# Scores of the second layer from fp16 halves of q and k, and the block of v ahead of the output block

## The chip, the cores and the metric

The kernel runs on one core of a Trainium2 chip. The engines that matter are TensorE (PE in the profile, PEld for its weight loads), VectorE (DVE), ScalarE (ACT), GpSimd (POOL) and SyncE (SP), whose queue issues every DMA. Each engine takes its own instructions strictly in the order in which they were written down and waits on semaphores for the others. The metric is the device time of one execution in microseconds (us); lower is better.

## The reference

128 graphs of 128 nodes with 512 features pass through two layers. Layer 0 is a graph layer with eight heads, which the change doesn't touch. Layer 1, which it does, is masked attention with four heads of 64 columns:

```python
h = jnp.maximum(_layernorm(x, axis=-1), 0.0)
q = split_heads(h @ Wq); k = split_heads(h @ Wk); v = split_heads(h @ Wv)
sim = jnp.einsum('bhid,bhjd->bhij', q, k) * scale
sim = jnp.where(adjacency_mask[:, None, :, :], sim, neg)
attn = jax.nn.softmax(sim, axis=-1)
out = jnp.einsum('bhij,bhjd->bhid', attn, v)
x = x + (out @ Wo + bo)
```

## The kernel before

`layer0` runs first and leaves its result in DRAM (`x_scratch`); `layer1` follows. In the profile its tiles carry the prefix `l_`.

A product of two float32 matrices is made from fp16 halves: each operand is scaled by a power of two and stored as a high half and the rest as a low half, and `split_products` adds high by high, high by low and low by high. The scores of layer 1 were the exception: `qk_copy` evicted q and k as float32 (`q_sb`, `k_sb`, scaled back by `unscale`), and `scores` (L1419) multiplied them as float32, four matmuls a graph, each for one head in half of the array's rows.

`layer1` goes over the graphs in one software-pipelined loop, written out by hand in each engine's own order. One step n handles several graphs at once:

- PE: `project_qk(n+4)`, 12 matmuls of 512 columns into `ps_pj[0]`, in turn a pair of heads of q or of k for a group of four graphs; `project_out(n-4)`, 6 matmuls of 512 columns; `scores(n+1)`; `project_v(n+4)`, 12 of 256 columns; `weigh_values(n-2)`, 12 small ones (L1432).
- ACT: `qk_copy(n+4)` (L1216 or L1218), `relu(n+10)` (L1204), `h_high(n+10)` (L1209), `exps(n+1)` (four exponentials with their sums, L1230), `v_high(n+4)` (L1224), `aT_high(n-2)` (L1242), `p_high(n+1)` (L1237).
- DVE: `add_residual(n-4)` (L1330), `row_max(n+1)` (four masked reductions in L121), `stats(n+15)` (L85, L87), `normalise(n+1)` (a reciprocal, L1311, and the product with it, L1313), `v_low(n+4)` (L1300), `aT_low(n-2)` (L1323), `p_low(n+1)` (L1318).
- POOL: `h_low(n+9)` (L1166), `add_bias(n-3)` (L1173), and in one step of four each `factors` (seventeen small operations, L102 to L105 with L74 to L80 between) and `convert_mask` (L1159).
- SP: `transpose_h(n+9)` (L1108), `transpose_p(n)` (L1115), the load of x for graph n+17 (L1098), in one step of four a load of masks (L1140), and `store(n-5)` (L1102). In steps with n%4 = 3 the transpose of p goes ahead of that of h.

`add_residual(n)` writes `o_sb[:, n % 2]` and so waits until the store of graph n-2 has landed. `ps_pj[0]`, `ps_pj[1]`, `ps_s`, `ps_av` and `ps_o` have one buffer each. The next block of q or k waits until the one before has left `ps_pj[0]`.

Of the kernel before, what the change touches and what calls it, by code (L numbers as in the profile page):

```python
# [26 lines left out]
HB = 4  # L27
# [89 lines left out]
def mask_scores(nc, dve, s_ready, n, masked, scores, mask, negmax):  # L117

    dve.wait_ge(s_ready, n)
    for i in range(HB):  # L120
        last = nc.vector.tensor_tensor_reduce(masked[:, i], scores[:, i // 2, (i % 2) * P:(i % 2 + 1) * P], mask, -1.0,  # L121
                                              FLOAT_MAX, ALU.add, ALU.min, negmax[:, i:i + 1])
    return last
# [44 lines left out]
def layer0(nc, next_layer, next_weights, x, adj, map_w, map_wT, map_b, q_wT, q_b, k_wT, k_b, gmap_w, gmap_b, gcn_WT, x1):  # L168

    with ExitStack() as ctx:  # L170
# [449 lines left out]
        def _(dve):  # L620
# [387 lines left out]
def layer1(nc, prepared, x1, adj, bo, out):  # L1008


    with ExitStack() as ctx:
# [6 lines left out]
        def sem(name):  # L1018
# [12 lines left out]
        q_sb = sb("q_sb", [P, 2, PAIRS1, QUAD * P])  # L1031
        k_sb = sb("k_sb", [P, 2, PAIRS1, QUAD * P])
# [15 lines left out]
        nprobs = sb("nprobs", [P, HB, P])  # L1048
# [24 lines left out]
        relu_done, hhi_done, q_done, k_done, vhi_done, exp_done, phi_done, ahi_done = act_sems = [  # L1073
            sem(n) for n in ("relu_done", "hhi_done", "q_done", "k_done", "vhi_done", "exp_done", "phi_done", "ahi_done")]
        hlo_done, vlo_done, negmax_done, rec_done, np_done, plo_done, alo_done, out_done = dve_sems = [
            sem(n) for n in ("hlo_done", "vlo_done", "negmax_done", "rec_done", "np_done", "plo_done", "alo_done", "out_done")]
        mask_ready, res_ready = pool_sems = [sem("mask_ready"), sem("res_ready")]
# [71 lines left out]
        def _(pool):  # L1149
# [25 lines left out]
            factors(QUAD)  # L1175
            convert_mask(0)
# [19 lines left out]
        def _(act):  # L1196
# [14 lines left out]
            def qk_copy(i):  # L1211

                g, c = divmod(i, QUAD)
                act.wait_ge(qk_ready, count(i + 1))
                if c % 2 == 0:
                    nc.scalar.activation(q_sb[:, g % 2, c // 2], ps_pj[0][:], ACT.Copy, scale=unscale["q"]).then_inc(q_done, 1)  # L1216
                else:
                    nc.scalar.activation(k_sb[:, g % 2, c // 2], ps_pj[0][:], ACT.Copy, scale=unscale["k"]).then_inc(k_done, 1)  # L1218
# [15 lines left out]
            def p_high(n):  # L1234
                act.wait_ge(np_done, count(n + 1))
                act.wait_ge(pT_loaded[n % 2], 16 * (n // 2))
                nc.scalar.activation(p16[:, n % 2, 0], nprobs[:], ACT.Copy, scale=F16_SCALE).then_inc(phi_done, 1)  # L1237
# [15 lines left out]
            act.wait_ge(scale_chain, SCALE_STEPS * len("qkvo") + 2)  # L1253
            for c in range(QUAD):
                qk_copy(c)
                v_high(c)
                relu(QUAD + c)
                h_high(QUAD + c)
# [6 lines left out]
            for n in range(B):  # L1265
                if n + QUAD < B:
                    qk_copy(n + QUAD)
# [5 lines left out]
                if n + QUAD < B:  # L1273
                    v_high(n + QUAD)
# [8 lines left out]
        def _(dve):  # L1283
# [12 lines left out]

            def v_low(i):
# [4 lines left out]
            def row_max(n):  # L1302
                if n % QUAD == 0:
# [3 lines left out]
                            negmax[:, n % 2]).then_inc(negmax_done, 1)  # L1307
# [8 lines left out]
            def p_low(n):  # L1316
                dve.wait_ge(phi_done, count(n + 1))
                nc.vector.scalar_tensor_tensor(p16[:, n % 2, 1], nprobs[:], F16_SCALE, p16[:, n % 2, 0], ALU.mult,  # L1318
                                               ALU.subtract).then_inc(plo_done, 1)
# [24 lines left out]
            nc.vector.tensor_tensor(unscale["o"], unscale["o"], unscale["v"], ALU.mult).then_inc(scale_chain, 1)  # L1344
            for n, k in enumerate("qkvo"):
# [3 lines left out]
            dve.wait_ge(scale_chain, SCALE_STEPS * len("qkvo") + 2)  # L1349
            for i in range(QUAD, 2 * QUAD):  # L1350
                stats(i)
            for j in range(QUAD):
                v_low(j)
# [3 lines left out]
            p_low(0)  # L1357
# [25 lines left out]
        def _(pe):  # L1383
# [3 lines left out]
            def project_qk(i):  # L1387
# [4 lines left out]

                if c % 2 == 0:
                    pe.wait_ge(k_done, count(2 * g + c // 2))
                else:
                    pe.wait_ge(q_done, count(2 * g + c // 2 + 1))
# [12 lines left out]
            def scores(n):  # L1409
                g, j = divmod(n, QUAD)  # L1410
                cols = slice(j * P, (j + 1) * P)
                if j == 0:
                    pe.wait_ge(q_done, count(2 * g + 2))
                    pe.wait_ge(k_done, count(2 * g + 2))
# [42 lines left out]
            for n in range(B):  # L1457
                if n + QUAD < B:
                    project_qk(n + QUAD)
                if n >= 4:  # L1460
# [3 lines left out]
                if n + QUAD < B:  # L1464
                    project_v(n + QUAD)
# [52 lines left out]
```

## Time and profile before

| | us |
|---|---|
| time, median of 3 runs | 2706.66 (2703.7 to 2708.87) |
| the profiled execution, its own time | 2705.26 |
| its span | 2703.5 |
| PE busy in the span | 2603.0 (96%) |
| DVE busy | 1982.0 (73%) |
| ACT busy | 1752.0 (65%) |
| POOL busy | 1404.3 (52%) |

The span is the time between the first and the last instruction that the profiler saw. A busy PE is not one at its peak. The mean over the span mixes both layers; layer 1 begins at about 1814 us and its steady part fills the stretch from about 1885 to 2665 us.

### The profile page before, as it was taken

To read this page: it belongs to the slowest core of one execution; us is meant where nothing else is said; L and a number is where in the kernel's file an instruction comes from. 1 tells how busy PE (TensorE), PEld (TensorE's weight loads), DVE (VectorE), ACT (ScalarE), POOL (GpSimd) and SP (SyncE) were. 2 spreads that over 40 slices of the span, in tenths; PEclk is the share of its full clock that TensorE was granted. 3 is DMA by queue.
4 is the path that set the end of the run, shared out by engine and by line. 5 is a ranking of instruction groups with operands and counts; after the bars stand their busy time and mean duration, and the time that the engine had idled before them with its cause. 6 is when DMAs were issued, how large, how long until landed. Compare 5 with 4: busy or idle time off the path is not lost. (4 is left out here: it accounts for less than half of the span.)

```text
span 2703.5 us, 62497 instructions
## 1 busy us (share of the span) xinstructions
PE 2603.0 (96%) x20886; PEld 1401.6 (52%) x20886; DVE 1982.0 (73%) x6359; ACT 1752.0 (65%) x5020; POOL 1404.3 (52%) x2798
## 2 busy tenths in 40 slices
PE   6999999999999999999999999947999999999998
PEld 3455555555555555555555555534555555555554
DVE  5487777777777877777777778755777777777765
ACT  3466666666666666666666666645777777777774
POOL 4255555455545555555555455514655556565552
PEclk8999999999999999999999999968999999999998
DMA  4257666766766676667666766575777778777763
GB/s 139 60 129 151 146 132 142 152 134 134 144 148 136 132 150 149 128 132 157 141 134 140 154 129 130 120 175 113 158 165 159 172 164 167 164 159 171 159 144 90
DMA packets 944336, 385.33 MB, mean 143 GB/s; under 512 B 857488, under 2 KB 859024, under 8 KB 944016
## 3 DMA queue, kind: packets, MB, share of 16 engines
q1 hardware_dynamic: 944016, 381.34, 66.2%
q8 instruction: 167, 2.74, 0.4%
q14 instruction: 153, 1.25, 0.1%
HBM read 112.76 MB, written 67.11 MB: 67 GB/s over the span
## 5 line engine op out<-in xcount | busy, mean ns | idle before, releaser
L534 ACT ACTIVATE probs<-probs,negmax 128x128 f32<-128x128 f32 x1024 | 398.2, 390 | 468.3 <-DVE negmax L121 468.3
L445 POOL TENSOR_TENSOR o_sb<-o_sb,xres 128x512 f32<-128x512 f32 x128 | 162.7, 1271 | 503.6 <-DVE o_sb L694 498.3
L163 PE MATMUL ps_pj<-wm_hi,hT 128*128 128x512 f16 x1024 | 325.1, 379 | 4.1 <-DVE m_sb L637 4.1
L163 PE MATMUL ps_pj<-wv_hi,hT 128*128 128x512 f16 x1024 | 326.4, 380 | 0.0
L163 PE MATMUL ps_pj<-hT,wk_hi 128*128 128x512 f16 x1024 | 305.8, 380 | 0.0
L163 PE MATMUL ps_pj<-hT,wq_hi 128*128 128x512 f16 x1024 | 305.3, 380 | 0.0
L1230 ACT ACTIVATE l_probs<-l_probs,l_negmax 128x128 f32<-128x128 f32 x512 | 199.1, 390 | 152.9 <-DVE l_negmax L121 152.9
L1166 POOL TENSOR_TENSOR l_h<-l_h 128x512 f16<-128x512 f32 x124 | 143.5, 1158 | 269.4 <-ACT l_h L1209 157.8
L121 DVE CUSTOM_DVE_ANT_0 probs<-ps_sc,mask 128x128 f32<-128x128 f32 x1024 | 235.4, 284 | 53.2 <-PE ps_sc L899 52.5
L676 DVE SCALAR_TENSOR_TENSOR c<-cprobs,c 128x512 f16<-128x512 f32 x256 | 182.9, 714 | 80.9 <-ACT c L541 80.8
L541 ACT ACTIVATE c<-cprobs 128x512 f16<-128x512 f32 x256 | 160.3, 626 | 118.4 <-DVE cprobs L670 114.7
L1173 POOL TENSOR_TENSOR l_xres<-room,l_bo_rows 128x512 f32<-128x512 f32 x124 | 169.2, 1364 | 63.4 <-DVE l_o_sb L1330 63.2
L670 DVE SCALAR_TENSOR_TENSOR cprobs<-ps_sc,bound,probs 128x512 f32<-128x512 f32 x256 | 189.1, 739 | 16.4 <-ACT probs L534 13.1
L632 DVE TENSOR_TENSOR h<-h 128x512 f16<-128x512 f32 x128 | 109.0, 851 | 122.2 <-ACT h L500 122.1
L892 PEld LDWEIGHTS ps_sc<-room 64*128 64x128 f32 x2048 | 135.9, 188 | 116.0 <-issue 115.8
L892 PE MATMUL ps_sc<-room 64*128 64x128 f32 x2048 | 185.2, 300 | 9.7 <-DVE cprobs L670 9.2
L163 PE MATMUL ps_pj<-hT,wq_lo 128*128 128x512 f16 x512 | 194.3, 379 | 0.0
L163 PE MATMUL ps_pj<-hT,wk_lo 128*128 128x512 f16 x512 | 194.0, 379 | 0.0
L163 PE MATMUL ps_pj<-wv_lo,hT 128*128 128x512 f16 x512 | 194.0, 379 | 0.0
L163 PE MATMUL ps_pj<-wm_lo,hT 128*128 128x512 f16 x512 | 194.0, 379 | 0.0
L163 PE MATMUL l_ps_pj<-l_wv_hi,l_hT 128*128 128x256 f16 x1024 | 190.5, 274 | 2.6 <-DVE l_v_lo L1300 2.5
L534 ACT ACTIVATION_READ_ACCUMULATOR probs<-probs,negmax 128x1 f32 x1024 | 191.0, 186 | 0.0
(197 smaller groups left out, 6675.8 us busy)
## 6 DMA issues: line engine op xcount, KB each, us to landing
xg<-in_x SPq DMA_DIRECT2D x128, 256.0 KB, 3.3
xres<-in_x SPq DMA_DIRECT2D x128, 256.0 KB, 3.0
x_scratch<-o_sb SPq DMA_DIRECT2D x128, 256.0 KB, 2.4
out<-l_o_sb SPq DMA_DIRECT2D x128, 256.0 KB, 3.3
room<-x_scratch SPq DMA_DIRECT2D x124, 256.0 KB, 3.1
cpT<-c SPq DMA_TRANSPOSE x256, 3.2
mask_u<-in_adj SPq DMA_DIRECT2D x32, 64.0 KB, 2.4
hT<-h SPq DMA_TRANSPOSE x128, 3.3
```

Of the source, the lines that this page charges most:

```text
L121: last = nc.vector.tensor_tensor_reduce(masked[:, i], scores[:, i // 2, (i % 2) * P:(i % 2 + 1) * P], mask, -1.0, FLOAT_MAX, ALU.add, ALU. ...
L163: last = pe.matmul(out, a(kt), b(kt), start=(n == 0), stop=(n == 3 * kts - 1))
L445: nc.gpsimd.tensor_tensor(o_sb[:, j % 2], o_sb[:, j % 2], xres[:, j % 2], ALU.add).then_inc(res_done, 1)
L534: last = nc.scalar.activation(probs[:, i], probs[:, i], ACT.Exp, bias=negmax[:, u % 2, i:i + 1], scale=-1.0, accum_out=zsum[:, u % 4, hh:h ...
L541: nc.scalar.activation(c16[:, n % 2, 0], cprobs[:], ACT.Copy, scale=F16_SCALE).then_inc(cph_done, 1)
L632: nc.vector.tensor_tensor(h16[:, j % 2, D:], h32[:, j % 2], h16[:, j % 2, 0:D], ALU.subtract).then_inc(hlo_done, 1)
L670: nc.vector.scalar_tensor_tensor(cprobs[:].rearrange("p (b h) n -> p b (h n)", b=2), ps_c[n % 2], bound[:, t % 2, j:j + 1], probs[:].rearr ...
L676: nc.vector.scalar_tensor_tensor(c16[:, n % 2, 1], cprobs[:], F16_SCALE, c16[:, n % 2, 0], ALU.mult, ALU.subtract).then_inc(cpl_done, 1)
L892: nc.tensor.matmul(ps_s[n % 2][:, b, pl * P:(pl + 1) * P], q_sb[rows, t % 2, pr, cols], k_sb[rows, t % 2, pr, cols], start=True, stop=True)
L1166: nc.gpsimd.tensor_tensor(h16[:, i % 2, D:], h32[:, i % 2], h16[:, i % 2, 0:D], ALU.subtract).then_inc(hlo_done, 1)
L1173: nc.gpsimd.tensor_tensor(xres[:, i % 2], row(i), bo_rows[:], ALU.add).then_inc(res_ready, 1)
L1230: last = nc.scalar.activation(probs[:, hh], probs[:, hh], ACT.Exp, bias=negmax[:, n % 2, hh:hh + 1], scale=-1.0, accum_out=zsum[:, n % 2, ...
```

## The change

Scores are made from fp16 halves. `qk_high` (ACT) writes the high half of a block of q or k as it stands in PSUM, `qk_low` (DVE) the rest, and `scores` issues twelve fp16 matmuls for the four float32 ones. The scale moves into `mask_scores`, where `score_scale` takes the place of -1.0, and into the mask, which now holds 0 or the scaled constant `excluded`. The next block on PE waits for `qk_low` (`qklo_done`) and no more for the copy.

`project_v`, `v_high` and `v_low` move: on PE ahead of `project_out`, on ACT ahead of `relu`, on DVE ahead of `add_residual`, right behind `qk_low`. `p_low` moves from DVE to POOL, behind `add_bias`. `normalise` gets one small operation more (it scales the sums before the reciprocal), `nprobs` a second buffer.

```diff
-                nc.gpsimd.tensor_scalar(mask[:, t % 2], mask_u8[:, t % 2], -NEG1, NEG1, ALU.mult, ALU.add).then_inc(mask_ready, 1)
+                nc.gpsimd.tensor_scalar(mask[:, t % 2], mask_u8[:, t % 2], -1.0, excluded[:, 0:1], ALU.add, ALU.mult).then_inc(mask_ready, 1)
@@ POOL
+            def p_low(n):
+                pool.wait_ge(phi_done, count(n + 1))
+                nc.gpsimd.tensor_tensor(p16[:, n % 2, 1], nprobs[:, n % 2], p16[:, n % 2, 0], ALU.subtract).then_inc(plo_done, 1)
...
                 if n >= 3:
                     add_bias(n - 3)
+                p_low(n)
                 if n % QUAD == 1 and n + 11 < B:
                     factors(n + 11)
@@ ACT
+                nc.scalar.copy(qk_hi["qk"[c % 2]][:, g % 2, c // 2], ps_pj[0][:]).then_inc(qkhi_done, 1)
...
             for n in range(B):
                 if n + QUAD < B:
-                    qk_copy(n + QUAD)
+                    qk_high(n + QUAD)
+                    v_high(n + QUAD)
                 if n + 10 < B:
                     relu(n + 10)
                     h_high(n + 10)
                 if n + 1 < B:
                     exps(n + 1)
-                if n + QUAD < B:
-                    v_high(n + QUAD)
@@ DVE
+            def qk_low(i):
+                g, c = divmod(i, QUAD)
+                kind = "qk"[c % 2]
+                dve.wait_ge(qkhi_done, count(i + 1))
+                nc.vector.tensor_tensor(qk_lo[kind][:, g % 2, c // 2], ps_pj[0][:], qk_hi[kind][:, g % 2, c // 2],
+                                        ALU.subtract).then_inc(qklo_done, 1)
...
             def normalise(n):
                 dve.wait_ge(exp_done, count(n + 1))
-                nc.vector.reciprocal(rec[:], zsum[:, n % 2]).then_inc(rec_done, 1)
-                dve.wait_ge(rec_done, count(n + 1))
-                nc.vector.tensor_tensor(nprobs[:], probs[:], rec[:].unsqueeze(2).to_broadcast([P, HB, P]),
+                dve.wait_ge(plo_done, count(n - 1))
+                nc.vector.tensor_scalar(rec[:], zsum[:, n % 2], 1.0 / F16_SCALE, None, ALU.mult).then_inc(rec_done, 1)
+                dve.wait_ge(rec_done, count(2 * n + 1))
+                nc.vector.reciprocal(rec[:], rec[:]).then_inc(rec_done, 1)
+                dve.wait_ge(rec_done, count(2 * n + 2))
+                nc.vector.tensor_tensor(nprobs[:, n % 2], probs[:], rec[:].unsqueeze(2).to_broadcast([P, HB, P]),
                                         ALU.mult).then_inc(np_done, 1)
...
             for n in range(B):
+                if n + QUAD < B:
+                    qk_low(n + QUAD)
+                    v_low(n + QUAD)
                 if n >= 4:
                     add_residual(n - 4)
...
                 if n + 1 < B:
                     normalise(n + 1)
-                if n + QUAD < B:
-                    v_low(n + QUAD)
                 if n >= 2:
                     aT_low(n - 2)
-                if n + 1 < B:
-                    p_low(n + 1)
@@ PE
-                if c % 2 == 0:
-                    pe.wait_ge(k_done, count(2 * g + c // 2))
-                else:
-                    pe.wait_ge(q_done, count(2 * g + c // 2 + 1))
+                pe.wait_ge(qklo_done, count(i))
...
                 for pr in range(PAIRS1):
-                    for b in range(2):
-                        rows = slice(DH * b, DH * b + DH)
-                        mm = nc.tensor.matmul(ps_s[:, b, pr * P:(pr + 1) * P], q_sb[rows, g % 2, pr, cols], k_sb[rows, g % 2, pr, cols],
-                                              start=True, stop=True)
+                    for i, (q_part, k_part) in enumerate(((qk_hi, qk_hi), (qk_hi, qk_lo), (qk_lo, qk_hi))):
+                        for b in range(2):
+                            rows = slice(DH * b, DH * b + DH)
+                            mm = nc.tensor.matmul(ps_s[:, b, pr * P:(pr + 1) * P], q_part["q"][rows, g % 2, pr, cols],
+                                                  k_part["k"][rows, g % 2, pr, cols], start=(i == 0), stop=(i == 2))
...
             for n in range(B):
                 if n + QUAD < B:
                     project_qk(n + QUAD)
+                if n + QUAD < B:
+                    project_v(n + QUAD)
                 if n >= 4:
                     project_out(n - 4)
                 if n + 1 < B:
                     scores(n + 1)
-                if n + QUAD < B:
-                    project_v(n + QUAD)
```

The set-up of layer 1 gains three small DVE operations for `score_scale` and `excluded`, for which POOL waits ahead of its first mask.

## Rows read from the trace of the kernel before

The numbers of graphs and steps follow from the code; the stretch is steady, and its steps repeat.

**Rows 1.** Windows: stretch, its length; busy PE, PEld, DVE, ACT, POOL; clock, DMA share, GB/s.

```profile
...
1850.00:1880.00 30.00, 20.82 (x125) 10.78 (x122) 16.41 (x60) 18.95 (x55) 16.45 (x42) 0.83 0.63 126
2300.00:2400.00 100.00, 100.00 (x782) 56.80 (x782) 72.92 (x248) 72.02 (x212) 59.08 (x103) 1.00 0.78 164
```

**Rows 2.** Chain that ended last, 2300 to 2330: start us, us, what.

```profile
...
2299.98 0.65 PE l_ps_s L1419 x8
2300.62 1.42 PE l_ps_pj L163 x12
2302.04 0.46 PE l_ps_av L1432 x12
2302.50 2.70 PE l_ps_pj L163 x12
2305.19 1.29 PE l_ps_o L163 x6
2306.49 0.65 PE l_ps_s L1419 x8
```

**Rows 3.** Timeline of DVE: start us, us, instruction, [idle before <-releaser].

```profile
...
2308.16 0.75 DVE L1330 SCALAR_TENSOR_TENSOR l_o_sb<-l_ps_o,l_w_st,l_xres 128x512 f32<-128x512 f32 x1 [2.41 <-DMA out<-l_o_sb]
2308.83 0.28 DVE L121 CUSTOM_DVE_ANT_0 l_probs<-l_ps_s,l_mask 128x128 f32<-128x128 f32 x1
...
2311.46 0.18 DVE L1311 RECIPROCAL l_rec<-l_zsum 128x4 f32<-128x4 f32 x1 [0.89 <-ACT l_probs L1230]
2311.68 0.69 DVE L1313 TENSOR_TENSOR l_nprobs<-l_probs,l_rec 128x512 f32<-128x512 f32 x1
2312.28 0.42 DVE L1300 TENSOR_TENSOR l_v_lo<-l_ps_pj,l_v_hi 128x256 f16<-128x256 f32 x1
2312.62 0.42 DVE L1323 SCALAR_TENSOR_TENSOR l_aT_lo<-l_ps_av,l_aT_hi 128x256 f16<-128x256 f32 x1
2313.06 0.69 DVE L1318 SCALAR_TENSOR_TENSOR l_p<-l_nprobs,l_p 128x512 f16<-128x512 f32 x1
2313.67 0.75 DVE L1330 SCALAR_TENSOR_TENSOR l_o_sb<-l_ps_o,l_w_st,l_xres 128x512 f32<-128x512 f32 x1
...
2317.19 1.06 DVE L1313 TENSOR_TENSOR l_nprobs<-l_probs,l_rec 128x512 f32<-128x512 f32 x1
```

**Rows 4.** Timeline of ACT, same stretch.

```profile
...
2309.78 0.40 ACT L1230 ACTIVATE l_probs<-l_probs,l_negmax 128x128 f32<-128x128 f32 x1 [2.51 <-DVE l_negmax L121]
...
2311.34 0.35 ACT L1224 CAST l_v_hi<-l_ps_pj 128x256 f16<-128x256 f32 x1
...
2312.40 0.63 ACT L1237 ACTIVATE l_p<-l_nprobs 128x512 f16<-128x512 f32 x1 [0.44 <-DVE l_nprobs L1313]
2312.94 0.67 ACT L1218 ACTIVATE l_k_sb<-l_ps_pj,l_w_st 128x512 f32<-128x512 f32 x1
2313.51 0.80 ACT L1204 ACTIVATE l_h<-room,ln_st 128x512 f32<-128x512 f32 x1
```

**Rows 5.** Waits of DVE, 2100 to 2500: total us, times, longest.

```profile
...
DVE l_o_sb L1330 <- DMA out<-l_o_sb: 38.2, 23, 3.1
```

**Rows 6.** Timeline of POOL, same stretch as 3.

```profile
...
2310.65 0.20 POOL L102 TENSOR_TENSOR ln_st<-ln_st,l_consts 128x4 f32<-128x4 f32 x1 [0.33 <-DVE ln_st L87]
...
2316.54 1.16 POOL L1166 TENSOR_TENSOR l_h<-l_h 128x512 f16<-128x512 f32 x1 [0.18 <-POOLq L108]
2317.66 1.72 POOL L1173 TENSOR_TENSOR l_xres<-room,l_bo_rows 128x512 f32<-128x512 f32 x1
...
2322.04 1.27 POOL L1173 TENSOR_TENSOR l_xres<-room,l_bo_rows 128x512 f32<-128x512 f32 x1
```

**Rows 7.** Timeline of the DMA queue on SP.

```profile
...
2304.71 0.42 SPq L1102 DMA_DIRECT2D out<-l_o_sb  x1
...
2313.78 1.23 SPq L1115 DMA_TRANSPOSE l_pT<-l_p  x1
...
2315.69 0.42 SPq L1102 DMA_DIRECT2D out<-l_o_sb  x1
```

More of the change, by code:

```diff
@@ L114, in slot, with mask_scores @@
     return 2 * (hh % 2) + hh // 2
-def mask_scores(nc, dve, s_ready, n, masked, scores, mask, negmax):
+def mask_scores(nc, dve, s_ready, n, masked, scores, mask, negmax, scale):
     dve.wait_ge(s_ready, n)
     for i in range(HB):
-        last = nc.vector.tensor_tensor_reduce(masked[:, i], scores[:, i // 2, (i % 2) * P:(i % 2 + 1) * P], mask, -1.0,
+        last = nc.vector.tensor_tensor_reduce(masked[:, i], scores[:, i // 2, (i % 2) * P:(i % 2 + 1) * P], mask, scale,
                                               FLOAT_MAX, ALU.add, ALU.min, negmax[:, i:i + 1])
@@ L1030, in layer1 @@
         bo_rows = sb("bo_rows", [P, D])
-        q_sb = sb("q_sb", [P, 2, PAIRS1, QUAD * P])
-        k_sb = sb("k_sb", [P, 2, PAIRS1, QUAD * P])
+        qk_hi = {k: sb(f"{k}_hi", [P, 2, PAIRS1, QUAD * P], F16) for k in "qk"}
+        qk_lo = {k: sb(f"{k}_lo", [P, 2, PAIRS1, QUAD * P], F16) for k in "qk"}
+        score_scale = sb("score_scale", [P, 1])
+        excluded = sb("excluded", [P, 1])
         v_hi = sb("v_hi", [P, 2, QUAD, INNER], F16)
@@ L1047, in layer1 @@
         probs = sb("probs", [P, HB, P])
-        nprobs = sb("nprobs", [P, HB, P])
+        nprobs = sb("nprobs", [P, 2, HB, P])
         p16 = sb("p16", [P, 2, 2, HB, P], F16)
@@ L1072, in layer1 @@
             sem(n) for n in ("qk_ready", "vp_ready", "s_ready", "av_ready", "o_ready")]
[L1073 to L1077, printed above, removed]
+        relu_done, hhi_done, qkhi_done, vhi_done, exp_done, phi_done, ahi_done = act_sems = [
+            sem(n) for n in ("relu_done", "hhi_done", "qkhi_done", "vhi_done", "exp_done", "phi_done", "ahi_done")]
+        hlo_done, qklo_done, vlo_done, negmax_done, rec_done, np_done, alo_done, out_done = dve_sems = [
+            sem(n) for n in ("hlo_done", "qklo_done", "vlo_done", "negmax_done", "rec_done", "np_done", "alo_done", "out_done")]
+        mask_ready, res_ready, plo_done = pool_sems = [sem("mask_ready"), sem("res_ready"), sem("plo_done")]
+        SCALE_OPS = SCALE_STEPS * len("qkvo") + 5
         adjt = adj.rearrange("(g j) p d -> g p j d", j=QUAD)
@@ L1209, in h_high, with qk_high @@
                 nc.scalar.copy(h16[:, i % 2, 0:D], h32[:, i % 2]).then_inc(hhi_done, 1)
-            def qk_copy(i):
+            def qk_high(i):
                 g, c = divmod(i, QUAD)
                 act.wait_ge(qk_ready, count(i + 1))
-                if c % 2 == 0:
-                    nc.scalar.activation(q_sb[:, g % 2, c // 2], ps_pj[0][:], ACT.Copy, scale=unscale["q"]).then_inc(q_done, 1)
-                else:
-                    nc.scalar.activation(k_sb[:, g % 2, c // 2], ps_pj[0][:], ACT.Copy, scale=unscale["k"]).then_inc(k_done, 1)
+                nc.scalar.copy(qk_hi["qk"[c % 2]][:, g % 2, c // 2], ps_pj[0][:]).then_inc(qkhi_done, 1)
             def v_high(i):
@@ L1236, in p_high @@
                 act.wait_ge(pT_loaded[n % 2], 16 * (n // 2))
-                nc.scalar.activation(p16[:, n % 2, 0], nprobs[:], ACT.Copy, scale=F16_SCALE).then_inc(phi_done, 1)
+                nc.scalar.activation(p16[:, n % 2, 0], nprobs[:, n % 2], ACT.Copy).then_inc(phi_done, 1)
             def aT_high(n):
@@ L1252, in _ @@
                 nc.scalar.activation(w_hi[k][:], raw[k], ACT.Copy, scale=w_st[:, n, 2:3]).then_inc(prep_hi, 1)
-            act.wait_ge(scale_chain, SCALE_STEPS * len("qkvo") + 2)
             for c in range(QUAD):
-                qk_copy(c)
+                qk_high(c)
                 v_high(c)
@@ L1306, in row_max @@
                 mask_scores(nc, dve, s_ready, count(n + 1), probs, ps_s, mask[:, n // QUAD % 2, n % QUAD],
-                            negmax[:, n % 2]).then_inc(negmax_done, 1)
+                            negmax[:, n % 2], score_scale[:, 0:1]).then_inc(negmax_done, 1)
             def normalise(n):
                 dve.wait_ge(exp_done, count(n + 1))
-                nc.vector.reciprocal(rec[:], zsum[:, n % 2]).then_inc(rec_done, 1)
-                dve.wait_ge(rec_done, count(n + 1))
-                nc.vector.tensor_tensor(nprobs[:], probs[:], rec[:].unsqueeze(2).to_broadcast([P, HB, P]),
+                dve.wait_ge(plo_done, count(n - 1))
[4 more added lines that the diff above has]
+                nc.vector.tensor_tensor(nprobs[:, n % 2], probs[:], rec[:].unsqueeze(2).to_broadcast([P, HB, P]),
                                         ALU.mult).then_inc(np_done, 1)
[L1316 to L1319, printed above, removed]
             def aT_low(n):
@@ L1352, in _ @@
             for j in range(QUAD):
+                qk_low(j)
                 v_low(j)
@@ L1356, in _ @@
             normalise(0)
-            p_low(0)
             for i in range(3 * QUAD, 15):
```

14 lines of the change are left out of this document (8 added, 6 removed).

## The prediction

> **What bounds the kernel now.** I read the windows first, for the stage that the change touches. In a steady stretch of layer 1 PE is busy all the time at the full granted clock, the other engines between 59 and 73% [rows 1]. The chain that ended last then stays on PE for whole steps: scores 0.65, the block of v 1.42, the weighing of values 0.46, the block of q or k 2.70, the output block 1.29. From scores to scores it is 2306.49 - 2299.98 = 6.51 us [rows 2]. PE is the bound there, and only there can the reader believe that cheaper matmuls pay.
>
> A bound by one busy engine hides loops in which several engines wait for each other in turn. So I looked next at DVE and ACT, in their timelines, for the shortest step that they can make. From the `add_residual` at 2308.16, which a store had held up, to the next at 2313.67 DVE needed 5.51 us and waited only for ACT's exponentials [rows 3]. That is a loop: add_residual, row_max, exps, normalise, p_high, p_low, add_residual. It lies 1.00 us under PE's step, and that slack is what swallows the waits for stores, 38.2 us in some 61 steps [rows 5]. Whether the change keeps this slack is the question.
>
> **PE's step after it.** Four float32 matmuls of scores, 0.65 us, become twelve fp16 ones of 128 columns. The nearest row from below is the weighing of values, also twelve of 128 columns in halves of the array: 0.46. From above, without any overlap of the halves: the output block's 6 x 512 columns in 1.29 us make 0.054 us for 128 columns, and twelve of them 0.65, as now [rows 2]. I take 0.46, since it is the same number and size of instructions. The order on PE changes no sum, except that the pause of about 0.1 us around the change to half-array matmuls may go. So PE's own step becomes 6.2 to 6.5 us; I take 6.3. Alone this would give (6.51 - 6.3) x 120 = 25 us. 120 is the number of steps with a block of q or k, 124, less some four of the ramp.
>
> **The loop through ACT and DVE after it.** In the new order ACT runs p_high(n), then qk_high(n+4); DVE's first work of the step is qk_low(n+4), which waits for it, and v_low, add_residual and row_max(n+1) are queued behind it. So the eviction of q and k and its low half come into the loop, and so does v_low, which before was done behind normalise while ACT made p_high. Only p_low leaves it. Start to start, from [rows 3, 4]:
>
> - p_high to qk_high: 0.54 (2312.40 to 2312.94).
> - qk_high to qk_low: 0.70. The eviction takes 0.67, and p_high's end to the start of p_low was 0.03.
> - qk_low to v_low: 0.67. The trace has no such operation. From below 0.61, a subtraction or product of 512 columns in SBUF (nprobs at 2311.68 to v_lo at 2312.28); from above 0.67, one of 512 columns out of PSUM (o_sb at 2308.16 to 2308.83). It reads PSUM, so 0.67.
> - v_low to add_residual: 0.34 (2312.28 to 2312.62). v_high is long done: it starts 0.57 after qk_high and takes 0.35, so it ends 0.92 after it, and v_low starts 1.37 after it.
> - add_residual to row_max: 0.67.
> - row_max to exps: 0.95 (2308.83 to 2309.78).
> - exps to DVE's first operation of normalise: 1.68 (2309.78 to 2311.46).
> - The added small operation and its wait: 0.22, as the reciprocal beside it (2311.46 to 2311.68); a second 0.22 for the reciprocal.
> - nprobs to p_high: 0.72 (2311.68 to 2312.40).
>
> The sum is 0.54 + 0.70 + 0.67 + 0.34 + 0.67 + 0.95 + 1.68 + 0.22 + 0.22 + 0.72 = 6.71 us. It is over PE's 6.3 and over the 6.51 of today, so the loop is the new bound and PE idles some 0.4 us a step. What stats, aT_low, relu and h_high cost stays hidden: stats behind the exponentials, aT_low behind p_high and qk_high, relu and h_high behind qk_low to row_max. The bounds of the loop are 6.60 (0.61 for qk_low, and 0.05 less for a plain copy, as p_high's 0.63 against 0.67) and 6.75.
>
> **What p_low on POOL does.** POOL was busy 59.08 in 100 us [rows 1], 3.85 a step; 1.16 more, the time of h_low, makes 5.0, so it doesn't become the bound. But one step in four it is late. Take a step n with n%4 = 1 and count from the start of p_high(n). p_low(n) runs from 0.66 to 1.82. The factors take 2316.54 - 2310.65 = 5.89 up to the next h_low [rows 6], so h_low starts at 7.76, add_bias at 8.88, p_low(n+1) at 10.18, and it ends at 11.34, where it was due at 6.71 + 1.82 = 8.53. On SP the transpose of p, the load and then the store are queued behind it; from the start of such a transpose to that of the store it is 2315.69 - 2313.78 = 1.91, and a store lands 2308.16 - 2304.71 = 3.45 after its start, which is when the waiting add_residual began [rows 3, 7]. So the store of graph n-4 has landed at 11.37 + 1.91 + 3.45 = 16.7. add_residual(n-2), which needs its buffer, is due two loops later at 2 x 6.71 + 0.54 + 0.70 + 0.67 + 0.34 = 15.7. A stall of 1.0 us in four steps, 0.25 a step, now with no slack to swallow it. In step n+2 the transpose of h goes behind that of p: p_low(n+2) ends at 16.0, two transposes of some 1.5 and a load of 0.6 bring the store to 19.6, landed at 23.1, and it is needed at 3 x 6.71 + 1.0 + 2.25 = 23.4. So there is no second stall, by 0.3 us. The moved block of v helps here: the transpose of h waited for it at times, and it now comes early. Bounds: 0 if stores land 1 us sooner, and 0.5 a step if a second step stalls too.
>
> **POOL beside DVE.** nprobs took 1.06 us in place of 0.69 while POOL's h_low and add_bias ran [rows 3, 6]. Late POOL work will meet one nprobs in four; 0.1 to 0.4 us each, so 0.05 a step. p_low itself meets qk_low and add_residual.
> The Trainium skill (SBUF — State Buffer, "Who interferes with whom") says that a DVE instruction with two SBUF inputs and a GpSimd instruction that reads SBUF take one read interface in turns, the second blocked until the first ends. By that rule nprobs would wait out up to 0.8 us of an h_low once in four steps, 0.2 a step in place of 0.05, and the time would be 18 us more, 2787. The row shows less, 0.37 in one nprobs.
>
> **The sum.** 6.71 + 0.25 + 0.05 = 7.01 us a step, 0.50 more than 6.51, x 120 = 60 us. Ramp and tail: PE waits for qk_low in the first group (about 0.2 x 3), the first p_low on POOL is 0.5 longer; the last steps lose v_low and p_low from their loop. Together +2, an estimate. The profiled execution's 2705.3 becomes 2767; the median is 1.4 above that execution, so 2769 us.
>
> **Rivals.**
> - The loop alone: no stall by stores, because they land sooner or POOL's lateness shrinks in the longer step. 6.60 to 6.75, x 120 and +2: 2720 to 2738 us. For it: the DMA share of 0.78 would fall, and the stall hangs on 1 us. Chance 0.23.
> - More stalls: the second store too, or nprobs blocked for a whole POOL operation, 7.2 to 7.4 a step: 2791 to 2815. PE's clock is part of this case: in the ramp, where PE waited, the granted clock was 0.83 [rows 1], and a stall of 1 us atop the 0.4 of idle could bring it down. Against: PE has slack then. Chance 0.15.
> - Faster. The loop does not bind, and PE's shorter step shows: 6.2 to 6.3, so 25 to 37 us less, 2670 to 2682. It decides at a loop under 6.5; that needs the qk part (0.54 + 0.70 + 0.67) to be dearer on paper than on the chip by 0.2 or more, if p_high and qk_high overlap further, say. Against it: each link is a start-to-start time out of the trace and each engine keeps its order. Chance 0.07.
> - No change: the loop comes out at 6.5 by small errors of both signs. 0.05.
> - The fp16 scores could also gain nothing (0.65). With the loop as bound this moves nothing.
>
> **How the numbers follow.** The forecast, loop with one stall, has 0.50: 2750 to 2790. I take 0.2% (5.4 us) as what can be told from no change. Slower: 0.50 + 0.23 + 0.15 = 0.88; same 0.05; faster 0.07. The range leaves out the faster and equal cases and the top of the third: 2720 to 2800.
>
> **What would show it.** In the changed profile PE is below 95% busy in steady windows and waits ahead of the q and k blocks for `qk_low`. DVE's steps without a stall are 6.7 us from add_residual to add_residual, with the waits for qk_high and for the exponentials in each. Behind each group of factors p_low on POOL comes late, and two steps on add_residual waits about 1 us for the DMA. Scores take 0.46. Steps of 6.2 to 6.3 with PE at 100% would prove the loop wrong; steps of 6.7 without the DMA wait would prove the stall wrong; qk_low much above 0.75 us would push the time over the range.

## The result

The changed kernel took 2781.44 us (2777.6 to 2789.28, six runs) against 2707.45 (2703.7 to 2709.93, six runs): a ratio of 1.0279, 95% interval 1.0267 to 1.0291. It is slower by 74 us, where 62 had been forecast (2769, range 2720 to 2800).

The windows of the changed kernel come first (stretch and length; busy PE, PEld, DVE, ACT, POOL; granted clock, DMA share, GB/s):

```profile
...
1850.00:1880.00 30.00, 20.89 (x150) 11.12 (x149) 15.76 (x55) 17.18 (x46) 14.81 (x39) 0.89 0.59 127
2300.00:2400.00 100.00, 90.18 (x770) 51.03 (x770) 73.43 (x248) 65.42 (x200) 67.55 (x115) 1.00 0.73 150
```

PE, which was busy without a pause [rows 1], is now busy for 90 of 100 us. No other engine is full. The time went into waits between engines. How long a step is now, read from `add_residual` to `add_residual` in DVE's timeline over 108 steps, from the first of these rows to the second:

```profile
...
1952.83 0.75 DVE L1339 SCALAR_TENSOR_TENSOR l_o_sb<-l_ps_o,l_w_st,l_xres 128x512 f32<-128x512 f32 x1
```

```profile
...
2723.91 0.74 DVE L1339 SCALAR_TENSOR_TENSOR l_o_sb<-l_ps_o,l_w_st,l_xres 128x512 f32<-128x512 f32 x1
```

(2723.91 - 1952.83) / 108 = 7.14 us. The same measure on the kernel before gives (2645.71 - 1941.87) / 108 = 6.52. The difference over 120 steps is 75 us; the two spans differ by 77.9. So the loss lies in the steady steps, and only 3 us elsewhere.

PE's own step did get shorter, as its timeline shows in a stretch in which PE was catching up after a wait and had none of its own (rows left out between are of the same blocks):

```profile
...
2299.89 0.60 PE L163 MATMUL l_ps_pj<-l_hT,l_wk_hi 128*128 128x512 f16 x2
...
2303.80 0.38 PE L163 MATMUL l_ps_o<-l_wo_hi,l_aT_hi 128*128 128x512 f16 x1
...
2305.19 0.23 PE L1427 MATMUL l_ps_s<-l_k_hi,l_q_hi 64*128 64x128 f16 x2
...
2305.63 0.30 PE L1440 MATMUL l_ps_av<-l_pT,l_v_hi 128*64 128x128 f16 x4
...
2306.09 0.61 PE L163 MATMUL l_ps_pj<-l_hT,l_wq_hi 128*128 128x512 f16 x2
```

From one block of k to the next block of q it is 2306.09 - 2299.89 = 6.20 us, and the twelve fp16 score matmuls hold PE for 2305.63 - 2305.19 = 0.44, where the float32 ones held it for 0.65 [rows 2]. That explains 0.21 of the 0.31 by which 6.20 is shorter than 6.51. The other 0.10 comes with the order of the blocks: e5 below has the new order with float32 scores and a median of 6.40 from block to block of q and k, e9 to e11 have fp16 scores with other orders and 6.30. What holds the step is on DVE and ACT. First DVE in a plain step:

```profile
...
2305.87 0.74 DVE L1339 SCALAR_TENSOR_TENSOR l_o_sb<-l_ps_o,l_w_st,l_xres 128x512 f32<-128x512 f32 x1
2306.53 0.34 DVE L121 CUSTOM_DVE_ANT_0 l_probs<-l_ps_s,l_mask,l_score_scale 128x128 f32<-128x128 f32 x1
...
2309.40 0.17 DVE L1323 TENSOR_SCALAR l_rec<-l_zsum 128x4 f32<-128x4 f32 x1 [0.89 <-ACT l_probs L1236]
2309.61 0.18 DVE L1325 RECIPROCAL l_rec<-l_rec 128x4 f32<-128x4 f32 x1
2309.82 0.69 DVE L1327 TENSOR_TENSOR l_nprobs<-l_probs,l_rec 128x512 f32<-128x512 f32 x1
2310.43 0.42 DVE L1332 SCALAR_TENSOR_TENSOR l_aT_lo<-l_ps_av,l_aT_hi 128x256 f16<-128x256 f32 x1
2311.68 0.69 DVE L1305 TENSOR_TENSOR l_q_lo<-l_ps_pj,l_q_hi 128x512 f16<-128x512 f32 x1 [0.84 <-ACT l_q_hi L1224]
2312.29 0.41 DVE L1311 TENSOR_TENSOR l_v_lo<-l_ps_pj,l_v_hi 128x256 f16<-128x256 f32 x1
2312.62 0.74 DVE L1339 SCALAR_TENSOR_TENSOR l_o_sb<-l_ps_o,l_w_st,l_xres 128x512 f32<-128x512 f32 x1
```

and ACT in the same step:

```profile
...
2307.72 0.40 ACT L1236 ACTIVATE l_probs<-l_probs,l_negmax 128x128 f32<-128x128 f32 x1 [1.19 <-DVE l_negmax L121]
...
2310.55 0.63 ACT L1243 ACTIVATE l_p<-l_nprobs 128x512 f16<-128x512 f32 x1 [0.91 <-DVE l_nprobs L1327]
2311.08 0.57 ACT L1224 CAST l_q_hi<-l_ps_pj 128x512 f16<-128x512 f32 x1
2311.55 0.38 ACT L1230 CAST l_v_hi<-l_ps_pj 128x256 f16<-128x256 f32 x1
```

From 2305.87 to 2312.62 it is 6.75 us. Going through the links in the order of the prediction: p_high to qk_high 0.53, to qk_low 0.60, to v_low 0.61, to add_residual 0.33, to row_max 0.66 (2305.87 to 2306.53), row_max to exps 1.19, exps to the small operation 1.68, then 0.21, 0.21 and 0.73. The sum is 6.75. DVE waits only for ACT in it (0.89 and 0.84) and ACT only for DVE (1.19 and 0.91), so there is no slack left in the loop.

The four steps of a group are not alike. In means over 27 groups they last 6.77, 6.76, 7.67 and 7.36 us; before it was 5.66, 6.39, 6.30 and 7.71, in which the shorter steps made up for the long one while PE went on without a pause. The third step is long by one instruction, in 23 of the 27 groups `nprobs`, in three the small operation ahead of it; the last group, shown further down, has neither. DVE:

```profile
...
2316.62 1.53 DVE L1327 TENSOR_TENSOR l_nprobs<-l_probs,l_rec 128x512 f32<-128x512 f32 x1
...
2320.26 0.74 DVE L1339 SCALAR_TENSOR_TENSOR l_o_sb<-l_ps_o,l_w_st,l_xres 128x512 f32<-128x512 f32 x1
```

nprobs takes 1.53 us in place of 0.69. POOL at that time:

```profile
...
2311.03 1.16 POOL L1169 TENSOR_TENSOR l_h<-l_h 128x512 f16<-128x512 f32 x1 [0.18 <-POOLq L108]
2312.15 1.29 POOL L1180 TENSOR_TENSOR l_xres<-room,l_bo_rows 128x512 f32<-128x512 f32 x1
2313.40 1.16 POOL L1174 TENSOR_TENSOR l_p<-l_nprobs,l_p 128x512 f16<-128x512 f32 x1
2314.54 0.69 POOL L1162 TENSOR_SCALAR l_mask<-l_mask_u,l_excluded 128x512 bf16<-128x512 uint8 x1
2315.20 1.16 POOL L1169 TENSOR_TENSOR l_h<-l_h 128x512 f16<-128x512 f32 x1
2316.31 1.29 POOL L1180 TENSOR_TENSOR l_xres<-room,l_bo_rows 128x512 f32<-128x512 f32 x1
```

The factors ended at 2311, and six operations follow without a gap, the last an `add_bias` from 2316.31 to 2317.60. nprobs started at 2316.62 and ended at 2318.15, 0.55 after POOL was done. As it takes 0.69 otherwise, it had done at most 0.14 of its work before. In means over the 27 third steps nprobs is 0.71 longer and the small operation 0.17, together 0.88 of the 0.91 by which that step exceeds a plain one.

The fourth step is long, 7.3 us or more, in 16 of 27 groups. The waits from 2100 to 2500 us (56 steps, 14 groups; total us, times, longest) name the place:

```profile
...
PE l_ps_s L1427 <- DVE l_k_lo L1305: 32.6, 14, 2.7
...
DVE l_o_sb L1339 <- DMA out<-l_o_sb: 3.5, 5, 1.1
DVE l_o_sb L1339 <- PE l_ps_o L163: 2.8, 6, 0.5
```

PE waits 2.3 us a group ahead of the scores of a new group, because these need the last low half of k, made in the same step. What follows, on PE (idle time ahead in brackets):

```profile
...
2461.82 0.23 PE L1427 MATMUL l_ps_s<-l_k_hi,l_q_hi 64*128 64x128 f16 x2 [2.27 <-DVE l_k_lo L1305]
...
2462.25 0.30 PE L1440 MATMUL l_ps_av<-l_pT,l_v_hi 128*64 128x128 f16 x4
...
2462.71 0.67 PE L163 MATMUL l_ps_pj<-l_hT,l_wq_hi 128*128 128x512 f16 x2
...
2463.60 1.06 PE L163 MATMUL l_ps_pj<-l_hT,l_wq_hi 128*128 128x512 f16 x2
...
2466.16 0.79 PE L163 MATMUL l_ps_pj<-l_hT,l_wq_hi 128*128 128x512 f16 x2
```

and in a window of 2 us of it (PEclk, the granted clock, is the first figure behind the busy times):

```profile
...
2464.00:2466.00 2.00, 2.00 (x6) 0.76 (x5) 1.01 (x5) 1.78 (x9) 1.16 (x1) 0.50 1.16 39
```

Two matmuls of the block of q take 1.06 us, where they took 0.60 above, at a granted clock of 0.50, the lower of PE's two levels (1.2 in place of 2.4 GHz), behind a wait of 2.27 us. (The DMA share, the next figure, reads above 1 in so short a window; nothing here rests on it.) Its eviction is not late yet, but the block of v and the output block behind it are, and `add_residual` pays:

```profile
...
2462.01 0.74 DVE L1339 SCALAR_TENSOR_TENSOR l_o_sb<-l_ps_o,l_w_st,l_xres 128x512 f32<-128x512 f32 x1
...
2469.81 0.75 DVE L1339 SCALAR_TENSOR_TENSOR l_o_sb<-l_ps_o,l_w_st,l_xres 128x512 f32<-128x512 f32 x1 [0.47 <-PE l_ps_o L163]
```

2469.81 - 2462.01 = 7.80 us. This does not happen in every group. PE waits 2.25 us or more in 26 of 27, but only in 11 of them did the granted clock fall, between 0.3 us ahead of the wait's end and 1.4 us behind it. Behind a wait of 2.27 us that ended at 2089.36 it stayed at 1.00, and that fourth step took 6.75. In nine of the eleven `add_residual` waited for the output block, and those steps last 7.68 in the mean. In seven other groups it waited for a store, and they last 7.86. The remaining eleven last 6.75 to 6.96. So the 0.60 by which the mean fourth step exceeds a plain one is made in about equal parts by PE's late blocks behind the wait and by stores.

The last of the 27 groups is a group without POOL's factors, since none are left to make. DVE, and PE at the next group's scores:

```profile
...
2690.15 0.74 DVE L1339 SCALAR_TENSOR_TENSOR l_o_sb<-l_ps_o,l_w_st,l_xres 128x512 f32<-128x512 f32 x1
...
2717.16 0.74 DVE L1339 SCALAR_TENSOR_TENSOR l_o_sb<-l_ps_o,l_w_st,l_xres 128x512 f32<-128x512 f32 x1
```

```profile
...
2716.97 0.23 PE L1427 MATMUL l_ps_s<-l_k_hi,l_q_hi 64*128 64x128 f16 x2 [1.38 <-DVE l_k_lo L1305]
```

(2717.16 - 2690.15) / 4 = 6.75: the third and fourth steps are as short as the plain ones. PE waits 1.38 in place of 2.27, 0.89 less, which is what the blocked instruction cost the third step, and the clock stays at 1.00. So 0.89 of PE's wait, too, comes from POOL's late chain. It is one group, and in it the loads of x have ended too and the transposes of h end; but e2 below, in which the third step has no blocked instruction, points the same way in the steady part, with 21.2 us of PE's waits in 14 groups, 1.5 each.

The forecast stall by stores is small: 3.5 us in 56 steps, 0.06 a step. It is also not where it was forecast. The late store of graph n-4 was to hold the `add_residual` that ends the third step, where 2 of 27 waited. The next one, which ends the fourth step and was ruled out by 0.3 us, waited in 7 of 27.

### The profile page after: what moved, and what is told of

It is laid out like the page before. It is cut to its first block and busy times, and to the rows that moved or that the text cites. A ratio compares the mean times of both kernels' runs of the same rounds, so it can differ in the third digit from the quotient of the medians.

```text
span 2781.4 us, 63904 instructions
## 1 busy us (share of the span) xinstructions
PE 2583.2 (93%) x21394; PEld 1389.7 (50%) x21398; DVE 2032.9 (73%) x6490; ACT 1735.2 (62%) x5020; POOL 1514.7 (54%) x2926
## 5 line engine op out<-in xcount | busy, mean ns | idle before, releaser
L1174 POOL TENSOR_TENSOR l_p<-l_nprobs,l_p 128x512 f16<-128x512 f32 x128 | 147.8, 1154 | 212.3 <-ACT l_p L1243 212.3
L163 PE MATMUL l_ps_pj<-l_hT,l_wq_hi 128*128 128x512 f16 x512 | 169.8, 416 | 23.0 <-DVE l_k_lo L1305 11.0
```

The lines of the kernel that those rows point to most:

```text
L163: last = pe.matmul(out, a(kt), b(kt), start=(n == 0), stop=(n == 3 * kts - 1))
L1174: nc.gpsimd.tensor_tensor(p16[:, n % 2, 1], nprobs[:, n % 2], p16[:, n % 2, 0], ALU.subtract).then_inc(plo_done, 1)
```

## The experiments

Each time was taken beside the kernel before on the same chip, whose median was 2705.4 for e1 to e4, 2708.2 for e5 to e8 and 2705.3 for e9 to e11. The four "steps" are means over 27 groups from DVE's timeline, as above; the same steps of the group in all kernels, in the order of the changed kernel, whose plain ones come first.

| | us | ratio to before, 95% | steps | mean |
|---|---|---|---|---|
| before | 2707.5 | | 5.66, 6.39, 6.30, 7.71 | 6.52 |
| changed | 2781.4 | 1.0267 to 1.0291 | 6.77, 6.76, 7.67, 7.36 | 7.14 |
| e1 constant scale | 2766.9 | 1.0206 to 1.0237 | 6.52, 6.53, 7.63, 7.31 | 7.00 |
| e2 p_low on DVE | 2782.0 | 1.0267 to 1.0297 | 6.89, 7.67, 6.89, 7.01 | 7.11 |
| e3 v back | 2801.3 | 1.033 to 1.0365 | 6.45, 6.51, 7.90, 8.22 | 7.27 |
| e4 no qk_low | 2767.1 | 1.0204 to 1.0243 | 6.48, 6.46, 7.91, 7.24 | 7.02 |
| e5 v first only | 2699.8 | 0.9954 to 0.9985 | 6.16, 6.81, 6.15, 6.95 | 6.52 |
| e6 filler | 2782.7 | 1.025 to 1.0281 | 6.81, 6.81, 7.61, 7.12 | 7.09 |
| e7 ahead | 2760.1 | 1.0169 to 1.0203 | 6.67, 6.75, 6.66, 7.56 | 6.91 |
| e8 mask early | 2773.6 | 1.0222 to 1.0253 | 6.77, 6.76, 7.43, 7.20 | 7.04 |
| e9 ahead, out first | 2700.3 | 0.9974 to 0.9993 | 5.85, 6.67, 5.86, 7.22 | 6.40 |
| e10 the same, store early | 2687.7 | 0.992 to 0.9957 | 6.57, 6.35, 6.31, 6.05 | 6.32 |
| e11 fp16 matmuls only | 2690.1 | 0.9923 to 0.9952 | 5.67, 6.24, 5.97, 7.50 | 6.35 |

**e1, the scale as a constant.** The masked reductions on DVE had become slower with the changed kernel's operand for the scale (344 ns against 284).

```diff
-                            negmax[:, n % 2], score_scale[:, 0:1]).then_inc(negmax_done, 1)
+                            negmax[:, n % 2], -1.0).then_inc(negmax_done, 1)
```

> The changed kernel with the constant -1.0 in the masked reductions in place of the operand score_scale; the scores are left unscaled. If the loop of DVE and ACT is the bound, the reduction's 0.27 us a head goes back to 0.21, the loop from 6.75 to 6.51, and the time falls by 0.24 x 120 = 29 us, to about 2752. If the step is set by PE, by the stores or by POOL, it moves by less than 8 us, to 2773 or more.

The plain step fell from 6.76 to 6.52, by just what the loop lost, yet the time only by 14.5 us. The first two steps gave 0.24 each, the third and fourth 0.04 and 0.05. The third still ends where POOL lets nprobs go (nprobs was blocked in 26 of 27 groups), and `add_residual` waited for a store in 12 of 27 fourth steps in place of 7. 0.24 in two steps of four is 0.12 x 120 = 14 us. So the loop sets two steps in four, and something that doesn't shrink with it holds the other two. My expectation had taken all four for the loop's.

**e2, p_low back on DVE.**

```diff
@@ DVE, behind aT_low(n - 2)
+                if n + 1 < B:
+                    p_low(n + 1)
@@ POOL, behind add_bias(n - 3)
-                p_low(n)
```

> The changed kernel with p_low back on DVE behind aT_low. Loop theory: qk_low then starts 1.27 us after p_high in place of 1.14, so the plain step is 6.88 in place of 6.75, and only what POOL's lateness costs (0.22 a step for the blocked nprobs, part of the 0.17 behind it) can come back: 2755 to 2775 us. Rival, that the slow p_low on POOL is the main cost: 2725 us or less.

2782 us, over the range that I had expected. Plain steps are 6.89, as the loop gives, 0.13 more. The excess over the plain step fell from 0.38 to 0.22 in the mean, 0.16 less, and the two cancel in the time. p_low on POOL is not the main cost, since POOL is late behind its factors without it too: in the second step the small operation and nprobs together now take 0.79 more.

**e3, the block of v back in its place.** The three moves of v undone on PE, ACT and DVE, all else kept.

> The changed kernel with the block of v, v_high and v_low back in their old places. Loop theory: v_low (0.33) leaves the loop, the plain step is 6.42; 40 us less if nothing else moves (2741), but the scores of a new group then stand closer behind the last block of q and k on PE and wait longer, which may take half of it back: 2741 to 2765 us. Rival, that moving v helps and its place costs nothing: 2781 us or more.

2801 us, outside the range of 2741 to 2765 and in the rival's (2781 or more). But the rival, by which the place of v costs nothing, is not borne out either: the plain step is 6.43 in the median, v_low's 0.33 less, as forecast. What took it back and more is that PE now stands before the scores of a new group earlier:

```profile
...
2300.76 0.23 PE L1429 MATMUL l_ps_s<-l_k_hi,l_q_hi 64*128 64x128 f16 x2 [3.33 <-DVE l_k_lo L1306]
```

3.33 us in place of 2.27, and add_residual waits for a store in 22 of 27 fourth steps, which last 8.22. The transpose of h, which stands ahead of the store, waited for `project_v` 13 times, 17.4 us in 400; the changed kernel has no such wait. Moving v was right by itself; here it hid part of the harm.

**e4, no qk_low.** `qk_low` is taken out, so the low halves of q and k are missing, and the waits for `qklo_done` become waits for `qkhi_done`.

> The changed kernel without qk_low: the low halves of q and k are left out and the twelve score matmuls all use the high halves. PE's work is the same. Loop theory: v_low now waits for v_high, the plain step is 6.41 in place of 6.75, and the scores of a new group wait 0.7 us less, so PE's clock holds: 2720 to 2740 us. Rival, that the low half is hidden and PE's matmuls or the stores set the step: 2775 us or more.

The plain step is 6.43 in the median, as expected from the wait for v_high. The time fell by 14 us and not by 41 to 61. The first two steps lost 0.3 each, the third grew by 0.24, since it is still held until POOL is done, and the fourth lost only 0.12, with a wait for a store in 18 of 27. The low half is in the loop: that is shown by the plain step. Its whole price is not.

**e5, only the move of v, on the kernel before.**

> The kernel before with nothing changed but the place of project_v, v_high and v_low, ahead of the output block and first in the step. v_low comes into the loop (it starts 1.49 us after p_high, when v_high has ended), which makes it 6.07 in place of 5.51, still under PE's 6.51. Loop theory: no change by more than 12 us, 2700 to 2719. Rival, that the move by itself is the harm: 2740 us or more.

2699.8 us, a little faster than before (0.9954 to 0.9985), just below the range given. The store waits, 38.2 us [rows 5], are down to 10.0 in the same stretch, as this row of its waits says:

```profile
...
DVE l_o_sb L1329 <- DMA out<-l_o_sb: 10.0, 13, 2.1
```

and its loop of 6.07 stays under PE's step, which is 6.40 in the median with this order. The mean step from DVE's timeline is 6.52, as before.

**e6, PE kept busy.** Nine matmuls into a spare bank ahead of the waiting scores.

> The changed kernel with nine matmuls of 512 columns into a spare bank, 1.94 us, ahead of the scores in the step in which these wait for the last low half of a new group (PE idle for 2.3 us or more there). If the lower clock behind that wait is what makes the next step long by PE (7.5 to 7.8 us in half of the groups), that part goes: 2766 to 2774 us, granted clock 1.00. If the clock costs nothing, 2781 us as before or more.

PE's timeline around the filler:

```profile
...
2459.81 2.11 PE L1475 MATMUL l_ps_fill<-l_wo_hi 128*128 128x512 f16 x9
2462.22 0.23 PE L1428 MATMUL l_ps_s<-l_k_hi,l_q_hi 64*128 64x128 f16 x2 [0.30 <-DVE l_k_lo L1306]
```

The clock from 2100 to 2500 us was 1.00 in place of 0.97, no `add_residual` waited for the output block any more, and the fourth step fell from 7.36 to 7.12. What is left of its length goes with waits for stores, in 10 of 27. But the time didn't fall (2782.7, where 2766 to 2774 had been expected). The 108 steps took 5.6 us less, and the first of them began 3.8 us later and the part behind them took 1.6 more. The lower clock is real and costs about a quarter of a microsecond in four steps in the profile; as a part of the time it is too small to be told.

**e8, the mask out of the late chain.**

```diff
-                if n % QUAD == 2 and n // QUAD + 1 < GROUPS:
+                if n % QUAD == 0 and n // QUAD + 1 < GROUPS:
                     convert_mask(n // QUAD + 1)
```

> The changed kernel with convert_mask (0.69 us on POOL) in the steps with n%4 = 0 in place of 2, so that it is not in POOL's late chain. If nprobs in the third step is held until POOL's late add_bias ends, that step goes from 7.64 to about 7.0, 19 us over 30 groups, and PE's wait and what follows it shrink too: 2745 to 2764 us. If the 0.84 of that nprobs has another cause, 2778 us or more.

2773.6 us; 8 less where 17 to 36 were expected. nprobs was 0.69 in every step, and yet the third step lasted 7.43. DVE and POOL show why:

```profile
...
2337.24 0.49 DVE L1323 TENSOR_SCALAR l_rec<-l_zsum 128x4 f32<-128x4 f32 x1 [0.90 <-ACT l_probs L1236]
...
2337.97 0.69 DVE L1327 TENSOR_TENSOR l_nprobs<-l_probs,l_rec 128x512 f32<-128x512 f32 x1
```

```profile
...
2336.41 1.29 POOL L1180 TENSOR_TENSOR l_xres<-room,l_bo_rows 128x512 f32<-128x512 f32 x1
```

The late `add_bias` now meets the small scaling operation, which takes 0.49 here in place of 0.17, ending as POOL ends. In the mean over the 27 third steps it takes 0.74, and 26 of them show it. The chain on POOL moved earlier and hit the instruction ahead. So nprobs's 0.84 was POOL's lateness, but this run took only 0.24 off the third step, because most of the block went to the small operation.

**e7, q and k one step ahead.** An attempt at a kernel in which the loop is short: `project_qk`, `qk_high` and `qk_low` for graph n+5, `qk_low` behind `row_max`, v as before, p_low on DVE.

```diff
@@ DVE
                 if n + 1 < B:
                     row_max(n + 1)
+                if n + QUAD + 1 < B:
+                    qk_low(n + QUAD + 1)
                 if n + 15 < B:
                     stats(n + 15)
```

> The fp16 scores kept, the rest rearranged: blocks of q and k one step earlier, qk_low behind row_max where DVE waits for the exponentials, v in its old place, p_low on DVE. By the loop theory ACT and DVE then need 5.94 us a step, PE 6.2, and PE is the bound again with no wait ahead of a new group's scores: 6.2 to 6.4 us a step, 2672 to 2695 us, faster than both. If the fp16 scores are themselves the harm, 2707 us or more.

2760 us, far over the expected 2672 to 2695. The first and third steps were 6.6 to 6.7 in place of 6.2. Its DVE and PE:

```profile
...
2302.54 0.68 DVE L1302 TENSOR_TENSOR l_k_lo<-l_ps_pj,l_k_hi 128x512 f16<-128x512 f32 x1
...
2307.45 0.75 DVE L1340 SCALAR_TENSOR_TENSOR l_o_sb<-l_ps_o,l_w_st,l_xres 128x512 f32<-128x512 f32 x1 [0.62 <-PE l_ps_o L163]
```

```profile
...
2303.37 0.59 PE L163 MATMUL l_ps_pj<-l_hT,l_wq_hi 128*128 128x512 f16 x2 [0.55 <-DVE l_k_lo L1302]
```

I had missed a chain across PE: qk_low (2302.54) lets `project_qk` start at 2303.37, `project_out` follows, `add_residual` waits for that until 2307.45, and row_max and the next qk_low are behind it. It waited so in 53 of the 54 first and third steps. In the second step nprobs is blocked by POOL again, in 25 of 27 groups.

**e9, the output block ahead of q and k on PE.** e7 with this, and with the scaling of the sums back in p_high and p_low.

```diff
@@ PE
-                if n + QUAD + 1 < B:
-                    project_qk(n + QUAD + 1)
                 if n >= 4:
                     project_out(n - 4)
+                if n + QUAD + 1 < B:
+                    project_qk(n + QUAD + 1)
```

> The version with q and k one step earlier, and on PE project_out ahead of project_qk, the scaling of the sums taken out of normalise again (in p_high and p_low as before). The chain that held it at 6.59 a step, qk_low, project_qk, project_out, add_residual, row_max, qk_low, loses project_out and add_residual. ACT and DVE need 5.73, PE 6.2. Without stalls 6.2 a step; the waits for stores now have 0.5 of slack in place of 1.0, so 6.3 to 6.5: 2681 to 2707 us. If the cross chain was not the bound, 2750 us or more.

2700.3 us, from 2760, in the range. The first and third steps are 5.75 in the median, DVE and ACT's own 5.73. With the second, 6.67, the first averages 6.26, and PE goes on without a wait at 6.30, so PE's step sets that pair. What is long is the fourth step, 7.22, with a wait for a store in 25 of 27.

**e10, the store ahead of the transpose of h.** In steps with n%4 = 3:

```diff
                 transpose_p(n)
+                early = n >= 5 and n + 9 < B and not first
+                if early:
+                    store(n - 5)
                 if n + 9 < B and not first:
                     transpose_h(n + 9)
```

> The same, and in the steps with n%4 = 3 the store goes ahead of the transpose of h in SP's queue. If the waits of add_residual for a store that stood behind that transpose are what is left, 10 to 20 us less than without it, 2670 to 2690 us; if not, the same.

2687.7 us, 12.6 less, in the range. Its window and its store waits over the same 400 us:

```profile
...
2100.00:2500.00 400.00, 399.50 (x3422) 218.52 (x3420) 363.69 (x1077) 296.64 (x888) 247.08 (x415) 1.00 0.80 170
```

```profile
...
DVE l_o_sb L1342 <- DMA out<-l_o_sb: 9.4, 15, 1.3
```

PE is full again, at 6.32 a step against its own 6.30, and this version, which leaves nothing out, is faster than both kernels: ratio 0.9938, 0.992 to 0.9957, to the kernel before.

**e11, the fp16 matmuls alone**, on the kernel before, with the low halves left out.

> The kernel before with nothing changed but the scores: q and k are evicted as fp16 and twelve fp16 matmuls a graph take the place of four float32 ones. The low halves are left out (the high half is multiplied three times), so there is no work on DVE for them. The loop stays at 5.51, PE's step falls from 6.51 to 6.2: up to 0.3 x 120 = 36 us less, less what the waits for stores take back with the smaller slack: 2672 to 2695 us. If the fp16 matmuls are themselves no gain, 2707.

2690.1 us, a ratio of 0.9923 to 0.9952, in the range. PE's step is 6.31 in the median and not 6.2, since the order of its blocks is the old one. The cheaper scores are worth 15 us where the loop has slack, less than the 0.20 x 120 = 24 of PE's step: `add_residual` waits for a store in 26 of 27 fourth steps.

## Why the prediction came out as it did

**The bound changes from PE to the loop of ACT and DVE: right.** 6.71 was forecast, 6.75 measured, but that the two are so close is luck: terms were off in opposite directions. row_max to exps was taken over from [rows 3, 4] as 0.95 and is 1.19, because I had put the new operand of the reductions at nothing; e1 shows that 0.24. Against it qk_high to qk_low was 0.60, not 0.70, qk_low to v_low 0.61, the lower bound, not 0.67, and the small links together 0.04 less. With the old reductions the loop would have been 6.51, just the step of before; e1 has that loop and is still 2.2% slower, by its third and fourth steps. The upper bound of 6.75 has no source in the prediction. e1 to e4 each moved the plain step to the length that the links give (6.52, 6.89, 6.43, 6.43), which no bound on PE, the stores or POOL would do.

**PE's 6.3: right, within its range of 6.2 to 6.5.** It is 6.20: 0.21 from scores of 0.44, which e11 shows by itself, and 0.10 from the order, which the prediction had named as possible and left out of the 6.3.

**The stall by stores, 0.25 a step: wrong as a term, and by the prediction's own sign.** Measured 0.06, and more at the second store, which had been ruled out by 0.3 us, than at the first. The first needed add_residual to be due 1.0 us before the store had landed, but nprobs, blocked in that same step, made it due 0.9 later. That this is why the first stall stayed away is argued from these times; no run shows it by itself.

**POOL beside DVE, 0.05 a step: the term that was mis-sized.** It is 0.23: the third step is 0.91 longer once in four. The reading of the row failed. nprobs with 1.06 at 2317.19 had started 0.51 before the end of POOL's h_low (2316.54 + 1.16 = 2317.70); its extra 0.37 was the wait for the rest of that operation and not a partial slowing, for it too ended 0.55 after POOL's operation (2317.19 + 1.06 = 2318.25). The `add_bias` queued behind took 1.72 in place of 1.27, 0.45 more, for the rest of nprobs [rows 3, 6]. Here nprobs met an `add_bias` that had begun 0.31 before, and waited for nearly all of it. The Trainium skill (SBUF — State Buffer, "Who interferes with whom") says that a DVE instruction with two SBUF inputs contends with a GpSimd instruction that reads SBUF, and that the second to start is blocked until the first ends. The trace agrees (1.53 in place of 0.69), and the 0.2 a step that was worked out beside the rule was the right size. The Trainium skill says in the same section that an instruction with at most one SBUF input outside the two-port modes doesn't contend, and that `tensor_scalar` can enter such a mode. The small operation of e8, a `tensor_scalar` with 0.49 in place of 0.17, agrees with the second.

That nprobs could be blocked for a whole POOL operation stood in the rival "more stalls", at 2791 us or more and a chance of 0.15. So the kernel did in part what that rival said, and the number came out in the forecast's range because the stall by stores wasn't there.

**What was not in the prediction.** The scores of a new group wait for a low half made in the same step: 2.3 us of PE's time a group, a granted clock of 0.50 at 11 of 26 such waits, and a late block of v and output block, for which 9 of 27 fourth steps wait. The rival on more stalls named PE's clock, not the place. These nine add 0.08 a step, and the seven fourth steps with a wait for a store 0.07, so the fourth step is 0.6 longer, 0.15 a step.

The sum that stands in place of the forecast's 6.71 + 0.25 + 0.05 = 7.01 is 6.76 + 0.23 + 0.15 = 7.14. The forecast was near by luck, because a term too large stood beside two too small or missing.

**Ramp and tail, +2:** 3 in the sum, measured. It is made up otherwise than forecast: the first of the 108 steps begins 11.0 us later than before, with eight steps and the ramp ahead of it, and the part behind them takes 0.3 us less.

What stays open: what the kernel would gain without POOL's late chain. The trace puts the third step's excess down to the blocked instructions, and the fourth's to PE's late blocks and to stores in about equal parts. e1 and e4 show that neither step shrinks with the loop, and e6 that the clock is a small part. The last group of the trace, without factors, runs at 6.75 in all four steps, but it is one group at the end of the loop. e2 and e8 moved POOL's chain and did not remove it, and e9 and e10 changed the loop as well, so no run shows what the whole kernel would gain.

## What to carry to other kernels

Before making the busiest engine cheaper, close each loop through the other engines in their written order, and see how much shorter than the bound it is; work moved ahead of a wait comes into that loop even if every engine has time to spare. Where steps come in groups of four, a saving in the plain step is paid out only in the plain ones. When the loop is the bound, look for an idle stretch inside it (here DVE waiting for the exponentials) and put the new work there, and then check the chain through the engine that consumes it.

## What the runs showed of the hardware that was not expected

A masked reduction of 128 x 128 on DVE took 344 ns with its scale read from a column in SBUF and 284 ns with a constant, start to start 0.27 against 0.21 us.

A DVE product with both inputs in SBUF that started while a 128 x 512 POOL elementwise operation ran took up to 0.84 us more than its 0.69; in the two rows read above it ended 0.55 after POOL's. POOL's operation was longer likewise when DVE was first (1.72 in place of 1.27). The profile shows this as a longer instruction and not as idle time before it, so its row has to be held against the other engine's.

PE's granted clock went to 0.50 in the matmuls at 11 of 26 waits of 2.25 to 2.7 us, and was 1.00 again within 5 us. At the other 15, of the same length, it stayed at 1.00, and so it did throughout the steady stretch with 2.1 us of dummy matmuls in the gap.
